# Two-layer graph product with LayerNorm on one core: loaded columns of the panel pairs as 2x2 blocks in seven products, with other orders of groups, turns and loads

## What is computed

```python
h = relu(layernorm(x))
u = par_u[0]*par_u[1] * (diag_u[:,None]*h[:2048] @ W_u) + h[:2048]
i = par_i[0]*par_i[1] * (diag_i[:,None]*h[2048:] @ W_i) + h[2048:]
e = concat(u, i)
g = adj @ (adj.T @ e)
out = x + (layernorm(g)*gamma + beta + h)
```

## Time and profile before

| | |
|---|---|
| median of three executions | 371.39 us |
| the profiled execution's own time | 371.32 us |
| its span, first to last instruction | 369.5 us |
| mean granted TensorE clock | 0.997 |
| PE / DVE / POOL / ACT busy | 98% / 71% / 43% / 20% |
| read from HBM | 131.55 MB |

### The profile page before, as it was taken

One profiled execution on the slowest core, in us unless ns is written; L12 is line 12 of the kernel. 1 busy time (PEld: TensorE's weight loads), 2 busy tenths in 40 slices (PEclk: granted clock), 3 DMA queues, 4 the chain that ended last, 5 costly groups with the idle time before them and its releaser, 6 DMA issues.

```text
span 369.5 us, 10865 instructions
## 1 busy us (share of the span) xinstructions
PE 360.3 (98%) x4776; PEld 151.7 (41%) x4776; DVE 263.0 (71%) x282; ACT 74.3 (20%) x213; POOL 159.6 (43%) x94
## 2 busy tenths in 40 slices
PE   7998999999999999999999999999999999999994
PEld 4664454543323443443334334334433343344432
DVE  5999994999061969395677839694956768385266
ACT  5863022010050004001300500040023005002422
POOL 2023060020019902970793199049607931990036
PEclk9999999999999999999999999999999999999998
DMA  8999999999999978989898989889898989853933
GB/s 311 422 419 415 418 426 419 419 419 402 403 380 411 363 291 331 427 343 411 323 429 331 419 326 425 338 318 421 349 409 326 427 339 413 325 247 132 426 130 142
DMA packets 19897, 133.22 MB, mean 361 GB/s; under 512 B 2209, under 2 KB 2977, under 8 KB 4001
## 3 DMA queue, kind: packets, MB, share of 16 engines
q1 hardware_dynamic: 19440, 132.22, 88.1%
q10 hardware_dynamic: 432, 0.66, 0.5%
HBM read 131.55 MB, written 1.31 MB: 360 GB/s over the span
## 4 chain that ended last, share of the span: by engine, by line
PE 87%; DMA 7%; POOL 2%; SPq 2%; DVE 1%; issue 0%; ACT 0%; DVEq 0%; POOLq 0%
PE h_acc L887 36%; PE t_acc L918 24%; DMA natural<-adj_rows 7%; PE x_acc L955 7%; PE h_acc L975 7%; PE t_acc L856 5%; PE t_acc L955 5%; PE h_acc L870 2%; POOL xs L424 1%; SPq L289 1%; POOL sums L420 1%; PE t_acc L993 1%; DVE xs L795 0%; SPq L286 0%; DVE sums L784 0%
## 5 line engine op out<-in xcount | busy, mean ns | idle before, releaser
L599 DVE STREAM_TRANSPOSE strips<-natural 128x2048 f32<-128x2048 f32 x76 | 169.0, 2279 | 48.2 <-PE h_acc L887 48.0
L887 PE MATMUL h_acc<-strips,tokens 32*64 32x512 f32 x2432 | 133.5, 589 | 0.1
L918 PE MATMUL t_acc<-natural,e 128*32 128x512 f32 x832 | 92.3, 592 | 0.1
L887 PEld LDWEIGHTS h_acc<-strips,tokens 32*64 32x64 f32 x2432 | 53.3, 132 | 79.4 <-issue 74.3
L399 POOL TENSOR_TENSOR sums<-natural 128x1024 f32<-128x1024 f32 x14 | 33.3, 2381 | 113.4 <-DMA natural<-adj_rows 113.4
L918 PEld LDWEIGHTS t_acc<-natural,e 128*32 128x32 f32 x832 | 27.4, 110 | 59.4 <-issue 58.2
L955 PE MATMUL x_acc<-sums,forms 128*32 128x256 f32 x280 | 41.1, 380 | 0.0
L856 PE MATMUL t_acc<-natural,e 128*64 128x256 f32 x320 | 36.5, 382 | 1.4 <-DMA natural<-adj_rows 1.1
L489 ACT COPY smalls<-x_acc 32x256 f32<-32x256 f32 x7 | 2.6, 365 | 170.1 <-PE t_acc L955 170.1
L479 ACT COPY tokens<-tokens 32x384 f32<-32x384 f32 (+2 forms) x60 | 24.2, 403 | 51.6 <-DVE tokens L623 30.9
L407 POOL TENSOR_TENSOR sums<-natural,sums 128x1024 f32<-128x1024 f32 x14 | 33.3, 2379 | 1.1
(11 more groups left out here) (97 smaller groups left out, 299.8 us busy)
## 6 DMA issues: line engine op xcount, KB each, us to landing
natural<-adj_rows SPq DMA_DIRECT2D x100, 1024.0 KB, 7.9
cols<-adj_cols SPq DMA_DIRECT2D x20, 1024.0 KB, 11.6
natural<-adj_last SPq DMA_DIRECT2D x4, 1024.0 KB, 10.8
out<-xs SPq DMA_DIRECT2D x4, 256.0 KB, 2.0
xs<-x ACTq DMA_DIRECT2D x2, 256.0 KB, 5.3
xs<-x SPq DMA_DIRECT2D x2, 256.0 KB, 7.7
out<-xs SPq DMA_DIRECT2D x2, 128.0 KB, 2.0
smalls<-small SPq DMA_DIRECT2D x1, 150.0 KB, 3.6
```

Of the source, the lines that this page charges most:

```text
L599: nc.vector.transpose(strips[:, a, :, m].rearrange("p c t i -> p t c i"), natural[:, a, m].rearrange("p t (c j) -> p t c j", j=Q)).then_in ...
L887: last = nc.tensor.matmul(h_acc[D * s:D * (s + 1), q], t[part, a, b, u, :], rows, start=(isinstance(g, int) and g == 0 and b == 0 and u == 0),
L918: last = nc.tensor.matmul(t_acc[lane, pair_bank(half)].rearrange("p (a w) -> p a w", a=2), e[:, GT * m + 2 * k + s, Q * v:Q * (v + 1)], na ...
```

## The change

The loaded columns of a pair are multiplied as 2x2 blocks in seven products. For each of the pairs 2 to 8, POOL makes four sums of the two panels' column blocks (`add_cols`) and four combinations of `t` (`form_t`); PE does 28 matmuls of 256 columns (`loaded_pair`, BY_LANE). Four of the products add into the bank of the loaded fifth, each in its lane of 32 partitions, and the rest into `t_acc[:, 1]`. They stay there until the end, where DVE combines them (`combine_products`) after ACT has copied one bank. Before the loop DVE clears `t_acc[:, 1]` and the last lane (`clear_products`), whose content ACT has saved (`kept`).

The sums take the place in SBUF that the residual had. So the residual is written to the output tensor in HBM ahead of the refill of columns 4 and read back behind the last loads into buffers of `natural` that are free by then; POOL and DVE add to that copy.

The order of groups becomes 0, 1, 4, 3, 2, so `first_rest` does groups 4, 3, 2. The order of transposes becomes 0, 3, 1, 2 from panel 6 on; for panels 4 and 5 all eight transposes are made before `t` is gathered. On SP, columns 4 and 5 are loaded right behind groups of panels 4 and 5, and in the loop the order for panels g and g + 1 becomes: 0, 1 of g; 4 of both; 0 of g + 1; 3 of both; 2 of g; the columns of g - 2 and g - 1; 1, 2 of g + 1. The loaded product of panel 3 moves ahead of the first products of pair 2.

```diff
@@ -32,9 +32,10 @@
-ORDER = (0, 1, 4, 2, 3)
+ORDER = (0, 1, 4, 3, 2)
 EARLY = 2
-TURNS = (0, 1, 3, 2)
+FIRST_TURNS = (0, 1, 3, 2)
+TURNS = (0, 3, 1, 2)
...
@@ -46,7 +47,11 @@
-SCRATCH = 2048
+BY_LANE = ((((2, 0, 0), (2, 1, 0), (2, 0, 1), (2, 1, 1)), (1, 0, 0), (1, 0, 1), (7, 0, 0)),
+           (((3, 0, 0), (3, 1, 0), (3, 0, 1), (3, 1, 1)), (1, 1, 0), (1, 1, 1), (7, 0, 1)),
+           (((4, 0, 0), (4, 1, 0), (4, 0, 1), (4, 1, 1)), (6, 0, 0), (6, 0, 1), (7, 1, 0)),
+           (((5, 0, 0), (5, 1, 0), (5, 0, 1), (5, 1, 1)), (6, 1, 0), (6, 1, 1), (7, 1, 1)))
+SCRATCH = 256
...
@@ -195,7 +218,8 @@
         def turned_count(g, m):
 
-            return TURNED * g + (TURNS.index(m) if g >= PAIRED else m) + 1
+            turns = range(TURNED) if g < PAIRED else FIRST_TURNS if g < PAIRED + 2 else TURNS
+            return TURNED * g + turns.index(m) + 1
...
@@ -327,17 +363,28 @@
                     refill(g, m)
                 if g == 2:
                     load_cols(1)
-                if g < PAIRED:
-                    refill_cols(g)
+                if g == PAIRED:
+                    sp.wait_ge(s_res, GROUPS)
+                    sp.dma_start(out[:], xs[:]).then_inc(s_spilled, 16)
+                refill_cols(g)
             for g in range(PAIRED + 2, PANELS, 2):
+                if g == PAIRED + 2:
+                    for m in ORDER:
+                        for a in range(2):
+                            refill(g + a, m)
+                    continue
+                for m in range(EARLY):
+                    refill(g, m)
                 for a in range(2):
-                    for m in range(EARLY):
-                        refill(g + a, m)
-                for m in (4, 3, 2):
-                    for a in range(2):
-                        refill(g + a, m)
+                    refill(g + a, 4)
+                refill(g + 1, 0)
+                for a in range(2):
+                    refill(g + a, 3)
+                refill(g, 2)
                 for a in range(2):
                     refill_cols(g - 2 + a)
+                for m in (1, 2):
+                    refill(g + 1, m)
             refill_cols(LAST - 1)
             for m in range(TURNED):
                 sp.wait_ge(s_first, firsts_pair(LAST_HALF, m))
...
@@ -346,12 +393,14 @@
             load_cols(LAST)
+            sp.wait_ge(s_spilled, 16)
+            sp.dma_start(res[:], out[:]).then_inc(s_reloaded, 16)
             for m in range(TURNED):
                 sp.wait_ge(s_o_added, m + 1)
-                sp.dma_start(out[:, rows_of(m), :], xs[:, rows_of(m), :]).then_inc(s_out, 16)
+                sp.dma_start(out[:, rows_of(m), :], res[:, rows_of(m), :]).then_inc(s_out, 16)
             for part in range(2):
                 sp.wait_ge(s_o_done, part + 1)
-                sp.dma_start(out[:, last_rows(part), :], xs[:, last_rows(part), :]).then_inc(s_out, 16)
+                sp.dma_start(out[:, last_rows(part), :], res[:, last_rows(part), :]).then_inc(s_out, 16)
             sp.wait_ge(s_out, 16 * (GROUPS + 1))
 
         @block.gpsimd
...
@@ -407,10 +456,47 @@
-            pairs(pool, add_blocks)
+            def add_cols(half):
+
+                done = 4 * (half - FIRST_HALF)
+                for a in range(2):
+                    pool.wait_ge(s_cols[a], 16 * (half + 1))
+                nc.gpsimd.tensor_tensor(col_sum(0), col_block(1, 0), col_block(1, 1), ALU.add).then_inc(s_col_sums, 1)
+                pool.wait_ge(s_col_sums, done + 1)
+                nc.gpsimd.tensor_tensor(col_sum(2), col_block(0, 0), col_block(1, 0),
+                                        ALU.subtract).then_inc(s_col_sums, 1)
+                nc.gpsimd.tensor_tensor(col_sum(1), col_sum(0), col_block(0, 0), ALU.subtract).then_inc(s_col_sums, 1)
+                pool.wait_ge(s_col_sums, done + 3)
+                nc.gpsimd.tensor_tensor(col_sum(3), col_block(0, 1), col_sum(1), ALU.subtract).then_inc(s_col_sums, 1)
+
+            def form_t(half):
+
+                done = 4 * (half - FIRST_HALF)
+                low, high = (t[:, a, :, 0].rearrange("p b (v d) -> p b v d", v=2) for a in range(2))
+                pool.wait_ge(s_t, 2 * half + 2)
+                pool.wait_ge(s_loaded_done, 2 * half)
+                nc.gpsimd.tensor_tensor(t_forms[:, 0], low[:, :, 1], low[:, :, 0], ALU.subtract).then_inc(s_t_forms, 1)
+                nc.gpsimd.tensor_tensor(t_forms[:, 2], high[:, :, 1], low[:, :, 1], ALU.subtract).then_inc(s_t_forms, 1)
+                pool.wait_ge(s_t_forms, done + 2)
+                nc.gpsimd.tensor_tensor(t_forms[:, 1], high[:, :, 1], t_forms[:, 0],
+                                        ALU.subtract).then_inc(s_t_forms, 1)
+                pool.wait_ge(s_t_forms, done + 3)
+                nc.gpsimd.tensor_tensor(t_forms[:, 3], high[:, :, 0], t_forms[:, 1],
+                                        ALU.subtract).then_inc(s_t_forms, 1)
+
+            pool.wait_ge(s_spilled, 16)
+            pool.wait_ge(s_loaded_done, PAIRED)
+            add_cols(FIRST_HALF)
+            add_blocks(FIRST_HALF + 1)
+            form_t(FIRST_HALF)
+            with pool.Fori(FIRST_HALF + 2, LAST_HALF + 1) as half:
+                add_blocks(half)
+                form_t(half - 1)
+                pool.wait_ge(s_loaded_done, 2 * half - 2)
...
@@ -517,10 +605,14 @@
+            act.wait_ge(s_loaded_done, PAIRED)
+            nc.scalar.copy(kept, h_acc[P - Q:P, LOADED]).then_inc(s_kept, 1)
             act.wait_ge(s_first, firsts_pair(FIRST_HALF, ORDER[-1]))
             keep_pair_high(FIRST_HALF)
             spread_pair(FIRST_HALF)
             pairs(act, pair)
+            act.wait_ge(s_loaded_done, 2 * LAST_HALF)
+            nc.scalar.copy(products, t_acc[:, 1]).then_inc(s_products, 1)
 
             def square_out(m):
                 n = LATER + m
...
@@ -669,6 +761,44 @@
+
+            def clear_products():
+
+                dve.wait_ge(s_t_sum, PAIRED + 2)
+                nc.vector.memset(t_acc[:, 1], 0.0).then_inc(s_cleared, 1)
+                dve.wait_ge(s_kept, 1)
+                nc.vector.memset(h_acc[P - Q:P, LOADED], 0.0).then_inc(s_cleared, 1)
+
+            def combine_products():
+
+                def place(lane, part):
+                    return t_acc[lane_of(lane), 1, columns_of(part)]
+
+                fifths = h_acc[P - Q:P, LOADED]
+                two, three, four, five = (halfway[lane_of(v)] for v in range(4))
+                lanes = [combined[lane_of(v)] for v in range(4)]
+                dve.wait_ge(s_products, 1)
+                for h in range(2):
+                    nc.vector.tensor_tensor(two[:, columns_of(h)], place(2 + h, 0),
+                                            products[lane_of(h), 0:WIDE], ALU.add).then_inc(s_halfway, 1)
+                for h in range(2):
+                    dve.wait_ge(s_halfway, h + 1)
+                    nc.vector.tensor_tensor(three[:, columns_of(h)], place(2 * h, 1),
+                                            two[:, columns_of(h)], ALU.add).then_inc(s_halfway, 1)
+                for h in range(2):
+                    dve.wait_ge(s_halfway, h + 3)
+                    nc.vector.tensor_tensor(lanes[2][:, columns_of(h)], place(2 * h + 1, 1),
+                                            three[:, columns_of(h)], ALU.add).then_inc(s_halfway, 1)
+                nc.vector.tensor_tensor(lanes[1], fifths, two, ALU.add).then_inc(s_combined, 1)
+                for h in range(2):
+                    nc.vector.tensor_copy(lanes[0][:, columns_of(h)], place(h, 0)).then_inc(s_combined, 1)
+                dve.wait_ge(s_halfway, 6)
+                nc.vector.tensor_tensor(five, fifths, lanes[2], ALU.add).then_inc(s_halfway, 1)
+                dve.wait_ge(s_combined, 3)
+                nc.vector.tensor_tensor(h_acc[0:P - Q, LOADED], h_acc[0:P - Q, LOADED], combined[0:P - Q],
+                                        ALU.add).then_inc(s_cols_whole, 1)
+                dve.wait_ge(s_halfway, 7)
+                nc.vector.tensor_tensor(h_acc[P - Q:P, LOADED], five, kept, ALU.add).then_inc(s_cols_whole, 1)
 
...
@@ -751,11 +881,16 @@
                 centre_e(m)
-            turn_pair(FIRST_HALF, keep_t_plain)
+            for a in range(2):
+                for m in FIRST_TURNS:
+                    turn_strips(PAIRED + a, a, FIRST_HALF, m)
+            keep_t_plain(FIRST_HALF)
+            clear_products()
             with dve.Fori(FIRST_HALF + 1, LAST_HALF) as half:
                 turn_pair(half, keep_t_pair)
             turn_first(LAST_HALF)
             keep_t_pair(LAST_HALF)
+            combine_products()
             dve.wait_ge(s_strips_last, 1)
             for half in range(2):
                 nc.vector.tensor_copy(*strips_across(half, 2)).then_inc(s_o_high, 1)
...
@@ -957,32 +1092,49 @@
             def first_rest(half):
-                first_summed(half, 4)
+                for m in SUMMED:
+                    first_summed(half, m)
                 first_plain(half, 2)
```

(44 more changed lines are left out.)

39 lines of the change are left out of this document (33 added, 6 removed).

## The result

The changed kernel took 465.91 us (median of six executions, 464.37 to 467.45); the kernel before, beside it on the same chip, 371.65. The ratio is 1.2538, with an interval of 1.2509 to 1.2568. The prediction said 455, from 437 to 467. The profiled execution took 467.45 us with a span of 465.6, which is 96.1 more than before. The medians differ by 94.3, so sums taken from the two traces run some 1.9 us above that.

The account below looks back on a forecast made before the run. PE bounds the kernel now, with DMA the near neighbour; the change makes PE wait for group 1's refill. Sum: 371.3 + 3.4 front + 67.0 waits + 11.4 clock + 1.6 end = 454.7, so 455 us, range 437 to 467.

Parts of the forecast that it names:

- The step that decided: Pair loop: second panel's group 1 lands at 41.6, wanted at 29.97; PE stands 11.6 us a turn, 67.0 over six.
- By the transpose: Pair loop: group 1's refill, held by its transpose, would land at 23.52 + 9.5 + 4.7 = 37.7.
- By the loads ahead on SP: Pair loop: group 1's refill, behind both column loads on SP, would land at 26.54 + 2.2 + 3 x 2.48 = 36.2.
- By the queue: Pair loop: nine DMA transfers from group 4's refill at 17.07 bring group 1 in at 41.6, the latest arrival.
- the transpose alone sets the wait (432): Rival, pair loop: the queue keeps up, turns of 41.2 + 1.9, total 432 us; chance 0.12.
- POOL binds (400): Rival, pair loop: group 1 in place, POOL's transfers and 30.6 of work make turns of 37.8, total 400; chance 0.04.
- group 1 is never late (368.4): Rival, pair loop: group 1 lands before 29.97, PE stays the bound, seven times 0.41 come off, 368.4; chance 0.05.
- the 45 to 47 us that were named as a sign: Pair loop: turn length that would show the forecast right; turns near 33.4 with PE unbroken would show it wrong.
- the clock after the wait: Pair loop: group 1 restarts at a lower clock, 1.9 us a turn (bounds nothing and 3.43), 11.4 over six.
- The rival in which the clock holds (443): Rival, pair loop: the granted clock stays up through PE's waits, total 443 us; chance 0.15.
- The front: Ahead of the loop: residual write and columns 4 delay panel 5's refills, PE waits in two pieces, +3.4 (0.4 to 6.5).
- The end: Behind the loop: DVE's combination of the products waits for ACT's copy and takes 6.1, +1.6 us (0 to 4).

Follow-up runs that it names:

- experiment 3: Changed kernel with the two loads of columns behind the second panel's groups 1 and 2 on SP instead of ahead; 443.92 us, ratio 1.1939.
- experiment 1: Changed kernel with transposes 0, 1, 3, 2, one behind the t operations, second panel's group 1 loaded ahead of groups 3 and columns; 385.73 us.
- experiment 2: Kernel before with only the new order of transposes and the new order of loads in the loop; 457.83 us, ratio 1.2314.
- experiment 4: Changed kernel with 48 zero-weight matmuls behind group 0 of the pair after next in each of six turns; 449.34 us, ratio 1.2085.
- experiment 5: Kernel before with the change's front alone: residual written, columns 4 ahead of panel 5, columns 5 behind, panel 3's loaded product earlier, no read-back; 376.86 us.
- experiment 7: Kernel with group 1 in time and the front as before, plus ACT's products copy before its last spread, residual reloaded before last columns; 378.77 us.
- experiment 8: Kernel of 378.77 us, with the second panel's group 0 transposed ahead of the first panel's last group and loaded ahead of groups 4; 375.59 us.
- experiment 6: Kernel of 385.73 us, with pair 2's eight products and columns 4, 5 loaded as before, residual written inside the loop ahead of columns 6; 381.17 us.

## Why the prediction was right

**The bound and the place.** The step that decided, group 1's refill landing 41.6 us into the turn for a want at 29.97, came out at 41.8 for 30.7, and PE's wait at 11.18 for 11.6. Its three arrivals can be checked one by one. By the transpose, the refill was to go out at 33.0 (23.52 + 9.5) and did at 33.0; experiment 3 took the columns away and it landed at 37.8, forecast 37.7. By the loads ahead on SP, the columns were to go out at 26.54 and did at 26.6, so they did not hold the refill's issue back. By the queue it landed 4 us later than by the transpose: the refill of group 4, the first of the nine transfers counted, went out at 17.1 and landed at 21.9, and the other eight followed 2.49 apart. Experiment 3 thus rules out that the transpose alone sets the wait (432), and experiments 1 and 2 that POOL binds (400); that group 1 is never late (368.4) the trace itself rules out.

The working left out one wait. Counted in the same way, the refill of the second panel's group 0 lands at 26.7 (17.07 + 2.2 + 3 x 2.48) for a want at 26.54. It landed at 26.9, and PE waited 0.56 us for it. That is most of why PE wanted group 1 at 30.7 and not at 29.97. In the changed kernel it costs nothing, because it comes out of the long wait; in experiment 1 it is what is left of the loss in a turn.

The time lies only 1.1 us under the upper end of the range, and the turns above the 45 to 47 us that were named as a sign. The parts did not cancel one another: by the trace the loop came out 8.2 us above its forecast, the front 2.6 and the end 2.0.

**Six turns.** Forecast 67.0 + 11.4 = 78.4, measured 86.6. The mis-sized term is the clock after the wait. It was taken at 1.9 a turn from the one restart in the trace of before. Group 1 took 6.41, 6.14, 6.00, 5.56, 5.67 and 5.61 us in the six turns, 2.1 to 3.0 above 3.43, together 14.8 for 11.4; it stayed under the bound of 3.43 that "all of it at half pace" had set. Experiment 4's fall of 16.6 agrees: by the traces 14.8 in the loop, 1.6 at the end, where the 3.4 us at half clock near 447 are also gone, and 0.4 ahead of the loop. (Group 1 takes 3.64 there, as group 0 does behind its small wait, so some 0.2 a turn are not the clock's.) The rival in which the clock holds (443) falls with that. The rule of the Trainium skill that stood beside that rival (TensorE: Matmul & The Clock Gate, "HAM oscillation": bursts that begin cold because PE waited for DMA) is what the six low stretches of the loop show, one behind each wait.

**What remains of the loop.** Of the 8.2 us above the forecast, 0.2 are rounding and 3.4 the clock's. The first turn adds 1.8: group 1 began 43.4 us into it. The prediction had POOL end group 3's sums 2.2 us after PE wants them there, and had the queue swallow that. PE did wait 1.3 us for POOL, and the queue did swallow it: the refills of groups 4 went out 17.1 and 17.5 us into that turn, as in the third, and the second of them took 8.4 us to land in place of 6.9; behind it the transfers landed 2.5 us apart as ever, group 1's at 43.3. In experiment 2, where PE does not wait for POOL, the first turn is 49.7 us long too, and group 1's refill lands 43.1 us into it. In the other five turns group 1 began 0.3 to 1.1 us later than the 41.6 counted, 2.8 us together, of which 0.14 a turn lie between landing and first matmul. In the fourth, the latest of the five, it is again one transfer: the first of the nine took 5.5 us to land in place of 4.8. Why single transfers take longer no run here took apart.

**POOL.** Forecast 30.6 us a turn and hidden, measured 29.13 and hidden. The one price that was open, 0.5 for an operation on 128x64 between 0.15 and 1.25, was 0.32. The column sums ended 6.2 to 6.6 us into the next turn in the three turns looked at (forecast 9.9), for a want at 23.5.

**The front.** Forecast +3.4 with bounds 0.4 and 6.5, measured +6.0, which experiment 5 repeats without the rest of the change (+5.8 at the loop's start). The chain of waits of the kernel after, which answers to the earlier trace rows:

```profile
86.01 1.87 PE h_acc L1005 x8
87.88 1.65 issue
89.53 7.07 PE t_acc L1053 x64
96.60 2.87 issue
99.47 5.17 PE t_acc L1053 x32
```

The two waits foreseen are there and come to 4.5 us, 1 more than counted. What the step left out is the last row: 5.17 us for a group of 3.43. The prediction priced a restart in the loop, but none here, where its own waits implied one.

**The end.** Forecast +1.6 with bounds 0 and 4, measured +3.6. The timeline of DVE in the kernel after (start, length, line, idle before and its releaser), which answers to the earlier trace rows:

```profile
434.84 0.88 DVE L715 STREAM_TRANSPOSE tokens<-t_sum 32x256 f32<-32x256 f32 x2 [0.61 <-PE h_acc L1022]
438.55 0.87 DVE L782 TENSOR_TENSOR natural<-t_acc,natural 32x256 f32<-32x256 f32 x2 [2.82 <-ACT natural L615]
...
445.06 1.29 DVE L896 COPY natural<-h_acc 128x512 f32<-128x512 f32 x2
446.38 0.69 DVE L906 TENSOR_TENSOR natural<-t_acc,natural 128x512 f32<-128x512 f32 x1
450.12 0.69 DVE L906 TENSOR_TENSOR natural<-t_acc,natural 128x512 f32<-128x512 f32 x1 [3.04 <-PE t_acc L1145]
```

The combination waited for ACT's copy, 2.82 us, and took 6.5, forecast 6.1. It ended at 445.03; counted from the loop's end, DVE then reached the sum behind it 2.1 us later than before, forecast 1.6. The rest, 1.5, goes with the granted clock, which was 0.50 from 447.3 to 450.7: the second L906 stood 3.04 us for PE. What brought the clock down there no run shows. PE had waited 1.00 and 0.88 us just before it; in experiments 3 and 4 it waited as long at the same place (1.00 or 1.01, and 0.87), the clock stayed at 1.00, and the end took 56.2 us in place of 57.7. Experiment 7 got 2.4 us back by moving the copy and the reload together, so it does not say which of the two did it.

**The seven products.** Forecast 3.02 in place of 3.43 and swallowed: 3.01, swallowed; where nothing is late, in two turns of experiment 8, the 0.4 shows in full.

**The sum of what was tried alone:** orders 86.5 (experiment 2), front 5.3 (experiment 5), end about 2.4 (experiment 7) make 94.2, and the change measured 94.3. That is closer than the parts are known, and so in part luck: experiment 7 gave back less than the 3.6 us that the trace shows at the end, and the trace's own parts add up to 96.1. Left open is what would bring the products' 0.4 a turn through to the end, since the residual must go to HBM and back for them: experiment 8 all but hid the way out, but none hid the way back, which lies in the chain that ends last in experiments 1, 7 and 8.

## What to carry to other kernels

When PE's order of use changes, buffers must be released in that same order: follow each operand back through what frees its buffer, its place in the issuing queue, and all transfers ahead of it, and take the latest. Count so for every operand, also for one that seems just in time. A long wait on PE can cost a second time, in the work behind it: here each wait of 7 to 11 us in the loop did, and so did those of 2.75 to 2.87 us ahead of it, while one of 3.10 us did not (experiment 8). So a restart needs a price, with nothing as its lower bound, wherever the working implies such a wait, ahead of a loop as well as in it. A buffer freed by sending 1.3 MB to HBM and back is not free: the transfer comes out in PE's time where a refill that PE wants soon stands behind it (experiments 5 and 6), or where its own return ends last (experiment 8).

## What the runs showed of the hardware

- After PE stopped at 246.96 in the turn shown, the granted clock was still 1.00 up to 249.2; from 249.3 it was 0.50 until 263.0, which is 4.86 us into the restarted work. Behind a wait of 2.87 us ahead of the loop it was down as well, for 3.5 us, in a kernel whose loop is the one before (experiment 5). Behind a wait of 3.10 us in experiment 8 it stayed at 1.00.
- With matmuls whose weights are zero in the long waits, the clock stayed at 1.00 for 345 us unbroken (experiment 4), and the time fell by 16.6 us for work that does nothing.
- POOL's additions of 128x1024 took the same in the kernels before and after (2.38 us and 2.36), and 2.36 to 2.40 in experiment 1, where POOL works 29.6 us and DVE 24.1 of a turn of 34.3.
